# Second attention: where ScalarE copies the third turned unit of a quad

## The reference, cut to what matters

```python
# B = 16 sequences, s = 256, H = 16 heads of HD = 8
q, k, v = heads_split(x @ Wq), heads_split(x @ Wk), heads_split(x @ Wv)
q = q * cos + _rotate_half(q) * sin
k = k * cos + _rotate_half(k) * sin
scores = jnp.einsum('bhqd,bhkd->bhqk', q, k) / sqrt(HD) + bias      # bias by relative position and head
scores = jnp.where(causal, scores, jnp.float32(-1000000000.0))
...                                                                 # softmax(scores) @ v, then @ Wo
x = _layernorm(x + _L1_attn_ref(x, ...), axis=-1)
```

## Time and profile before

| | |
|---|---|
| Median of three runs | 2669.52 us (2665.9 to 2669.61) |
| The profiled execution | 2671.13 us, of which the span from the first to the last instruction is 2669.3 us |
| Stage 2 in the span | about 642 us to 931 us |
| Granted clock of PE, whole span | 0.947 of full speed |
| Busy, whole span | PE 87%, DVE 68%, PE's weight loads 68%, ACT 54%, POOL 51% |

### The profile page before, as it was taken

How to read it: one execution, slowest core, us unless ns; L and a number is a source line. 1 busy time by engine, 2 the same in 40 slices (tenths; PEclk the granted TensorE clock), 3 DMA queues, 4 the chain that set the end, 5 groups by cost and what they waited for, 6 DMA issues and landing times. The chain is left out here.

```text
span 2669.3 us, 72175 instructions
## 1 busy us (share of the span) xinstructions
PE 2316.6 (87%) x21404; PEld 1817.1 (68%) x21404; DVE 1826.1 (68%) x8013; ACT 1442.1 (54%) x3445; POOL 1353.3 (51%) x1540
## 2 busy tenths in 40 slices
PE   7999999697999817799997999589978999999986
PEld 5777777355676616677775777467757777777755
DVE  4777777566888734578886799756646777777646
ACT  2444454224777615477775566355546666666614
POOL 4787787003777543388883555323314544444501
PEclk9999999798999958899998999899989999999978
DMA  2000000421000025500001000000000000000001
GB/s 77 3 0 0 0 0 0 115 66 70 2 0 0 0 78 161 155 4 0 0 0 41 2 1 0 0 2 1 0 24 2 1 0 0 0 0 0 0 0 33
DMA packets 44039, 55.98 MB, mean 21 GB/s; under 512 B 6800, under 2 KB 29417, under 8 KB 43564
## 3 DMA queue, kind: packets, MB, share of 16 engines
q1 hardware_dynamic: 41580, 49.37, 6.4%
q0 software_dynamic: 2304, 4.79, 0.5%
HBM read 47.11 MB, written 9.74 MB: 21 GB/s over the span
## 5 line engine op out<-in xcount | busy, mean ns | idle before, releaser
L1116 POOL TENSOR_TENSOR a_sm<-a_sm,a_top 128x512 f32<-128x512 f32 x512 | 520.5, 1040 | 171.0 <-DVE a_top L910 170.9
L910 DVE CUSTOM_DVE_ANT_0 a_sm<-bank,cst 128x128 f32<-128x128 f32 (+1 forms) x1024 | 296.6, 353 | 100.7 <-PE bank L769 87.0
L1037 ACT ACTIVATE a_pr<-a_sm 128x512 f32<-128x512 f32 x512 | 310.4, 629 | 81.8 <-PE bank L783 47.6
L1047 ACT ACTIVATE a_pt<-bank 128x512 f32<-128x512 f32 x432 | 240.3, 591 | 142.5 <-PE bank L783 139.9
L2944 POOL TENSOR_TENSOR a_pr<-a_sm,a_rden 128x512 f32<-128x512 f32 x192 | 197.1, 1047 | 228.2 <-DVE a_rden L2730 221.9
L783 PE MATMUL bank<-cst,a_pr 128*128 128x128 f32 x2304 | 309.4, 278 | 0.4 <-ACT a_pt L1047 0.2
L783 PEld LDWEIGHTS bank<-cst,a_pr 128*128 128x128 f32 x2304 | 258.9, 142 | 30.1 <-issue 20.9
L803 PEld LDWEIGHTS bank<-a_pt,a_v 128*32 128x32 f32 x4608 | 118.4, 109 | 110.2 <-issue 88.7
L2704 DVE CUSTOM_DVE_ANT_0 a_sm<-bank,cst 128x256 f32<-128x256 f32 (+1 forms) x512 | 149.8, 353 | 52.5 <-PE bank L2588 45.2
L803 PE MATMUL bank<-a_pt,a_v 128*32 128x128 f32 x4608 | 155.7, 275 | 28.7 <-issue 21.4
L910 DVE CUSTOM_DVE_ANT_0 a_sm<-bank,bias 128x256 f32<-128x256 f32 (+1 forms) x512 | 146.2, 354 | 31.4 <-PE bank L769 29.1
(11 more groups left out here) (492 smaller groups left out, 5931.6 us busy)
## 6 DMA issues: line engine op xcount, KB each, us to landing
f_w<-in_l_w SPq DMA_DIRECT2D x40, 256.0 KB
f_spread<-gate_rows SPq DMA_DIRECT2D x16, 512.0 KB
W<-in_l_w SPq DMA_DIRECT2D x2, 2048.0 KB, 9.7
x_sorted<-in_l_blank SPq DMA_DIRECT2D x4, 660.0 KB, 7.4
f_xin<-x_sorted SPq DMA_DIRECT2D x10, 264.0 KB
X<-in_x SPq DMA_DIRECT2D x4, 512.0 KB, 7.0
bias<-bias_rows SPq DMA_DIRECT2D x1, 2048.0 KB, 8.1
X<-y_rows SPq DMA_DIRECT2D x8, 256.0 KB, 5.3
```

The costliest lines, as they stand in the source:

```text
L910: ins = dve.tensor_tensor_reduce(sm[j][:, m * kw:(m + 1) * kw], sbank[j][:, m * kw:(m + 1) * kw], mk, 1.0, 3.0e38, ALU.add, ALU.min, top[: ...
L1037: act.activation(pr[j][:, :], sm[j][:, :], ACT.Exp, scale=-1.0).then_inc(S["probs"], 1)
L1047: act.activation(pt[j][:, :], tbank[j % 2][:, :], ACT.Copy).then_inc(S[f"turned_out{j}"], 1)
L1116: pool.tensor_tensor(whole, whole, top[:, qt, a:a + m].unsqueeze(2).to_broadcast([P, m, kw]), ALU.subtract).then_inc(S["shifted"], 1)
```

## The change

On ACT, in stage 2, the copy of turned unit 2 of the quad before (c2) stands behind p0 and ahead of p1 and p2; before, it stood behind p2. In the slots behind the loop there are no exponentials of a new quad, and the copies keep their order. In the other narrow stages (`hd.thin` false) the copy stays where it was: the tuple there loses unit 3, which ACT never copied.

```diff
                 copies(i, s, (0, 1))
                 if in_loop(i):
                     probs(i, s, 0)
+                if hd.thin:
+                    copies(i, s, (2,))
+                if in_loop(i):
                     probs(i, s, 1)
                     steps_in(i, s, 2)
                     probs(i, s, 2)
-                copies(i, s, (2, 3))
+                if not hd.thin:
+                    copies(i, s, (2,))
                 if in_loop(i):
                     steps_in(i, s, 3)
```

## The result

| | before | after |
|---|---|---|
| Median (range) | 2669.57 us (2665.9 to 2672.43) | 2649.49 us (2648.49 to 2651.07) |
| Ratio | | 0.9925, 95% interval 0.9912 to 0.9938 |
| Span of the profiled execution | 2669.3 us | 2649.2 us |
| Stage 2, from its first values (L803) to the first instruction of the next stage | 652.84 to 933.15: 280.3 us | 652.93 to 914.05: 261.1 us |

The change saves 20.1 us where 15.6 were forecast: the forecast had 2653.9 and its range began at 2649.5, so the time lies at its very edge. The two profiled executions reach stage 2 at the same time, the stage takes 19.2 us less, and the program behind it 1.0 us less (1736.2 against 1735.2).

A forecast was written before the change was run, and what follows sets the result against it. PE was taken to bound stage 2, with one hole a sequence ended by c2. 15 holes by 0.95 us (14.3) and 1.3 at the loop's end give 15.6 us: 2653.9 us, range 2649.5 to 2662.5.

The forecast's parts named there:

- What bounds the stage, and what makes the hole: Stage 2 runs at PE's pace, with one 1.04 us hole a sequence ahead of slot A's values, ended by c2.
- c2 in slot C: In slot C c2 starts at 778.36, where p1 started, and the hole of 1.04 us goes whole.
- What is late next: Scores of slot B, also waiting for the product L928, start at about 783.95: a gain of 0.95 us a sequence.
- the forecast's sign of 16.3 to 16.4 us a sequence: Sign that the forecast is right: a sequence of stage 2 takes 16.3 to 16.4 us.
- POOL's chain: Slot C: POOL's work ahead of p0 and c2 still releases the values in time, by 0.1 to 0.3 us.
- The rival that priced this chain: POOL's chain comes last, moving half a microsecond a sequence instead of one: 8.8 us gained, 2660.7 us, chance 0.10.
- p1, p2 and p3 later at no cost: On ACT p1 and p2 come 0.5 us later, p3 does not move; cost nothing, up to 0.2 us a sequence uncovered.
- the forecast's sign of 0.2 us of idle time there: Sign that the forecast is right: ACT has a new idle time of about 0.2 us ahead of c2 in slot B.
- The end of the loop: Behind the loop c2 ends at 917.27 and the values start 1.3 us earlier; a kept-up clock counted as nothing.
- the 18.3 that the forecast took as the most: Largest gain in stage 2: the whole 16.2 us of waits plus 1.3 and 0.8 at the loop's end, 2651.2 us.
- DVE did not take over: Rival: scores and later waits in stage 2 follow DVE, 0.84 us a sequence, 13.9 us in all, 2655.6 us, chance 0.15.
- The clock did not fall in the full stretch: Rival: PE's granted clock in stage 2 falls from 1.00 to 0.91, 2677.9 us; slower (clock or ACT's queue) 0.05.

The follow-up runs named there:

- slots A and B alone: Changed kernel with the new order of c2 in slots A and B only, the old order in slot C: 2669.12 us, 0.9996 to the kernel before.
- c2 behind p1: Changed kernel with c2 of stage 2 one exponential later, behind p1 and ahead of p2: 2660.91 us, 0.9966 to the kernel before.
- a second copy: Changed kernel with one more copy, to a buffer nobody reads, directly ahead of c2 in slot C: 2656.86 us, 0.9946 to the kernel before.
- before, hole filled: Kernel before, old order, with 16 throwaway transposes on PE in the hole behind the loop: 2670.21 us, 0.9998 to the kernel before.

## Why the prediction was right, and which terms were off

- *What bounds the stage, and what makes the hole.* Right. The two runs that delay c2 by 0.80 and 0.48 us bring back a hole of 0.59 and 0.29 us, the run that moves c2 still further ahead gains nothing, and PE is busy 171.75 of 172 us.
- *c2 in slot C.* Right in its place: it follows p0 directly.
- *What is late next: 0.95 us a sequence.* The term that was mis-sized: it is 17.29 - 16.14 = 1.15, and the forecast's sign of 16.3 to 16.4 us a sequence was missed. The step took the end of L928 as fixed against the scores of slot A, 783.80 - 778.27 = 5.53 us, since masks follow scores, and so had the scores of B 783.95 - 778.27 = 5.68 us behind those of A. They come after 5.55 us (760.66 - 755.11). Ahead of L928 stands the residual L344, and that waits for PE's projection L816, which stood behind the hole. PE of the kernel before, and DVE of the changed one:

```profile
782.40 0.61 PE L816 MATMUL bank<-W,a_on 128*128 128x128 f32 x4
```
```profile
756.52 0.29 DVE L910 CUSTOM_DVE_ANT_0 a_sm<-bank,bias 128x128 f32<-128x128 f32 x1 [0.63 <-PE bank L769]
...
759.90 0.29 DVE L344 TENSOR_TENSOR X<-bank,X 128x128 f32 x1
760.10 0.41 DVE L928 TENSOR_TENSOR a_on<-a_osb,bank 128x256 f32<-128x256 f32 x1
```

  Before, the projection ended at 783.01 and the residual started at 783.18, 3.49 us behind the first mask; now it starts 3.38 behind it, as the 16 masks end. L928 ends 760.51 - 755.11 = 5.40 us behind the scores' start, and the 0.15 us from there to the scores of slot B lie within the 0 to 0.21 assumed. That gives 0.13 of the missing 0.20 us, by 15 about 2 us. Most of the rest is that the earlier trace rows show a sequence with a smaller hole: the scores of B come 6.63 us behind those of A there, and 6.73 in every other sequence. No run took the projection away from the residual, so the reading rests on these rows. That L928 holds the scores of B at all shows in 0.03 us only: they start 0.56 us behind the start of L1233 (760.10), and 0.53 in slot B (766.17 against 765.64), where no L928 stands ahead of them.
- *POOL's chain: a cover of 0.1 to 0.3 us.* Right: 0.15 us by the rows, 0.21 and 0.19 by the two runs. The rival that priced this chain did not come in.
- *p1, p2 and p3 later at no cost.* Right: with c2 ahead of p0 ACT waits 24 us more for its turns, 25 less elsewhere, and it costs nothing. The 0.18 us that c2 was to wait in slot B are 0.05 (764.40 + 0.52 against 764.97), as the turns come earlier; the forecast's sign of 0.2 us of idle time there did not show.
- *The moves in slots A and B.* Not priced at all, and this was a gap in the working: of the stage's gain 4.6 us hang on them, 3.6 of these on slot A, where POOL's third subtraction would have held p2 and c2. The forecast followed POOL's chain in slot C alone. It came out right because the change moved c2 in every slot, which is luck as far as the working goes.
- *The end of the loop: 1.3 us.* Mis-sized. The hole shrank by 2.21 - 0.95 = 1.26, as worked out; the clock, for which the range had 0 to 0.8 and the sum nothing, gave 1.6. The 0.8 counted the eight turns alone, but PE ran slow until past 923 us.
- *The sum.* From its first values to the last of the loop the stage takes 912.57 - 652.84 = 259.7 us before and 896.32 - 652.93 = 243.4 after, 16.3 less; with 1.26 and 1.6 at the end that is 19.2 us, and the last microsecond lies outside the stage. The 16.3 are 1.09 a sequence and not 1.15, since one microsecond is lost once, where the first pass, which the kernel writes out, goes over into the loop proper: in both kernels ACT waits 1.7 us there ahead of p3, and in the changed one the turns of PE behind it wait 1.14 us for ACT (677.97) where they waited 0.16. What holds ACT there is open. Of the shortfall of 4.5 us, 2.1 are the loop, 1.5 the end with its clock, 0.9 the rest of the program. All of them fell to the same side: the stage alone gained 19.2 us, more than the 18.3 that the forecast took as the most, and the range reached this far only by the 1.7 us it had for the spread of the runs. So the cause was right, and that the time still lies in the range was in part luck.
- *The rivals.* DVE did not take over: it is busy 155.26 of 172.00 us now, 90%, its idle times of 0.43 and 0.41 us are gone, and PE is still busy nearly all the time. The clock did not fall in the full stretch (1.00); its part was the reverse, at the loop's end.

The Trainium skill (PSUM — Partial Sum Buffer, Engine vs sequencer instructions) says that ScalarE's queue is strictly first in, first out. The runs agree, p1 to p3 stood behind the waiting c2, and they add the price here: nothing, with readers that come a slot later.

## What to carry to other kernels

Order a queue by who waits for each result, not by where its input comes from: a copy whose reader is the bound engine goes ahead of exponentials whose readers come a slot later. When a hole in the bound engine is closed, follow the next slot too, since a release that was just in time there becomes the new hole; and of a term "this end does not move" check every wait in front of it for one that comes from behind the hole.

## What the runs showed of the hardware

What PE's clock did behind the one long hole at the loop's end, in six runs:

| run | hole, us | eight turns behind it, us | granted clock there |
|---|---|---|---|
| slots A and B alone | 2.26 | 1.97 | 0.50 (918 to 921 us) |
| before | 2.21 | 1.84 | 0.50 (920 to 923 us) |
| c2 behind p1 | 1.75 | 1.09 | 1.00 (910 to 913 us) |
| a second copy | 1.44 | 1.09 | 1.00 (907 to 910 us) |
| after | 0.95 | 1.09 | 1.00 (902 to 905 us) |
| before, hole filled | 0.48 | 1.09 | 1.00 (920 to 923 us) |

Of the two levels, 1.00 is 2.4 GHz and 0.50 is 1.2 GHz. The repeated holes of 1.0 to 1.2 us in the loop never lowered the clock (1.00 from 660 to 900 us). I had left the clock out of the sum for want of a row between the two, and the run with 1.75 us is one: with that hole the fall was already gone. Each of these is one profiled execution, and what a hole of such a length does elsewhere is not shown.
